# A fused attention and mixture-of-experts layer: squares stored head by head, and the first row maximum ahead of their sums

## What is computed

```python
h = layernorm(x) * (1 + ca) + sa              # ca, sa, ga, cb, sb, gb: per batch, from silu(c) @ wmod
Q, gate = split(h @ Wq + bq); K = h @ Wk + bk; V = h @ Wv + bv      # 16 heads of 8 features
Q = qn_w * Q * rsqrt(mean(Q*Q over a head's 8) + 1e-6); K likewise with kn_w
attn = softmax(Q @ K.T / sqrt(8)); o = (attn @ V) * sigmoid(gate)
x = x + ga * (o @ Wo + bo)
h = layernorm(x) * (1 + cb) + sb
x = x + gb * (top-2 of 32 experts, each a 128 x 128 matrix, weighted by the softmax of h @ router_w.T)
```

## Time and profile before

| what | us |
|---|---|
| median of 3 runs | 1000.58 |
| lowest, highest | 999.42, 1006.95 |
| the profiled execution | 1003.27 |
| its span in the profile | 1001.5 |
| VectorE busy in it | 741.2 |
| the square sums (L1103), 32 times | 32.5 |
| the row maxima (L1134), 512 times | 337.0 |

### The profile page before, as it was taken

One profiled execution on the slowest core, in us unless ns is written; L12 is line 12 of the kernel. 1 busy time (PEld: TensorE's weight loads), 2 busy tenths in 40 slices (PEclk: granted clock), 3 DMA queues, 4 the chain that ended last, 5 costly groups with the idle time before them and its releaser, 6 DMA issues. The chain is left out here.

```text
span 1001.5 us, 25119 instructions
## 1 busy us (share of the span) xinstructions
PE 650.4 (65%) x5838; PEld 412.3 (41%) x5839; DVE 741.2 (74%) x2240; ACT 539.7 (54%) x1335; POOL 545.1 (54%) x887
## 2 busy tenths in 40 slices
PE   3278798888889889888888888887187850000000
PEld 1135455555555545555554555554086740000000
DVE  8388799999999999999998999973334823334433
ACT  1247687777788878787877787875023320000000
POOL 7122255666566666666665666656600007677775
PEclk9569999999999999999999999998589995555555
DMA  2635564545444635454455445432188863444443
GB/s 70 189 86 142 129 155 127 157 119 141 123 124 125 141 112 138 122 142 118 122 133 130 121 119 137 116 97 62 35 262 273 271 210 89 111 115 104 115 115 89
DMA packets 128433, 132.33 MB, mean 132 GB/s; under 512 B 16900, under 2 KB 112868, under 8 KB 128388
## 3 DMA queue, kind: packets, MB, share of 16 engines
q1 hardware_dynamic: 100868, 95.81, 37.1%
q0 software_dynamic: 8192, 16.79, 6.2%
q10 hardware_dynamic: 19328, 19.20, 5.8%
HBM read 78.62 MB, written 52.56 MB: 131 GB/s over the span
## 5 line engine op out<-in xcount | busy, mean ns | idle before, releaser
L1134 DVE TENSOR_REDUCE negmax<-mx_ps 128x2 f32<-128x512 f32 x512 | 337.0, 682 | 25.2 <-PE mx_ps L1488 24.6
L884 ACT ACTIVATE pr<-st_ps 128x512 f32<-128x512 f32 x512 | 287.7, 596 | 41.9 <-PE st_ps L1512 41.7
L1488 PE MATMUL mx_ps<-k_aug,q_aug 126*128 126x256 bf16 x1024 | 195.4, 278 | 88.8 <-DVE negmax L1134 51.1
L748 POOL DMA_INDIRECT yg<-ys_d,gi x128 | 124.8, 975 | 147.6 <-DMA ys_d<-ys 101.9
L1512 PE MATMUL st_ps<-q_aug,k_aug 128*128 128x256 bf16 x1024 | 169.7, 273 | 0.9 <-ACT pr L884 0.4
L706 POOL DMA_INDIRECT xs_d<-h,slot x128 | 127.7, 998 | 55.8 <-DVE slot L1257 31.9
L1488 PEld LDWEIGHTS mx_ps<-k_aug,q_aug 126*128 126x128 bf16 x1024 | 75.2, 97 | 190.8 <-issue 182.2
L1526 PE MATMUL o_ps<-pr,v_aug 128*32 128x256 f32 x2048 | 138.8, 389 | 0.4 <-issue 0.4
L1512 PEld LDWEIGHTS st_ps<-q_aug,k_aug 128*128 128x128 bf16 x1024 | 92.0, 100 | 34.7 <-issue 12.6
L1388 DVE TENSOR_SCALAR yw<-yg,p_all 128x128 f32<-128x128 f32 x64 | 16.4, 314 | 113.7 <-DMA yg<-ys_d,gi 113.7
L1526 PEld LDWEIGHTS o_ps<-pr,v_aug 128*32 128x32 f32 x2048 | 53.9, 110 | 50.0 <-issue 28.4
(11 more groups left out here) (168 smaller groups left out, 1261.2 us busy)
## 6 DMA issues: line engine op xcount, KB each, us to landing
q_aug<-q_d SPq DMA_DIRECT2D x64, 192.0 KB
xs<-xs_d SPq DMA_DIRECT2D x96, 128.0 KB, 3.0
ys_d<-ys ACTq DMA_DIRECT2D x48, 256.0 KB, 3.0
mod_o<-mod_d SPq DMA_DIRECT2D x32, 256.0 KB, 4.8
bias_p<-bias_d SPq DMA_DIRECT2D x32, 200.0 KB, 4.8
q_d<-parts SPq DMA_DIRECT2D x32, 192.0 KB, 2.1
k_d<-parts SPq DMA_DIRECT2D x32, 192.0 KB, 2.1
k_aug<-k_d SPq DMA_DIRECT2D x64, 96.0 KB
```

The lines of the kernel that those rows point to most:

```text
L748: nc.gpsimd.indirect_dma_start(yg[:, par, k, :], None, ys_d, bass.IndirectOffsetOnAxis(ap=gi[:, par, k:k + 1], axis=0)).then_inc(yg_ld[par ...
L884: nc.scalar.activation(pr[:, h % PR], st_ps[score_bank(b, h)][:], ACT.Exp, scale=SCALE).then_inc(exp_d, 1)
L1134: v.tensor_reduce(negmax[:, :, h], mx_ps[h % 2][:], AX.X, ALU.max, negate=True).then_inc(mx_d, 1)
L1488: last = t_.matmul(mx_ps[h % 2][:, qc], q_aug[b.par][0:MROW, h, qc * P:(qc + 1) * P], k_aug[b.par][0:MROW, h, :], start=True, stop=True)
```

## The change

ScalarE squares the two halves of 128 tokens one by one, and writes a head's eight squares side by side: it reads Q and K as before and writes with a step of 8 elements (32 bytes) between neighbours. VectorE's sum then reads packed elements, and writes `ss` in the same order as before. In VectorE's order the first row maximum of the next batch stands in front of the sum instead of behind it. Nothing else moves.

```diff
             def squares(b):
                 wait(act, qkv_d, TB * (b.n + 1))
                 wait(act, ss_d, b.n)
-                nc.scalar.activation(sq[:], qkvg[:, b.par, :, 0:2 * P], ACT.Square).then_inc(sq_d, 1)
+                for t in range(TB):
+                    ins = nc.scalar.activation(sq[:, t].rearrange("p (k h d) -> p k d h", k=2, h=H),
+                                               qkvg[:, b.par, t, 0:2 * P].rearrange("p (k d h) -> p k d h", k=2, h=H), ACT.Square)
+                ins.then_inc(sq_d, 1)
...
             def square_sums(b):
                 wait(dve, sq_d, b.n + 1)
-                v.tensor_reduce(ss[:].rearrange("p (k h) -> p k h", h=H),
-                                sq[:].rearrange("p t (k d h) -> p (t k) h d", k=2, h=H), AX.X, ALU.add).then_inc(ss_d, 1)
+                v.tensor_reduce(ss[:],
+                                sq[:].rearrange("p t (g d) -> p (t g) d", d=HD), AX.X, ALU.add).then_inc(ss_d, 1)
...
                 ln2_stats(b4)
                 ln2_aggregate(b4)
+                max_head(b1, 0)
                 square_sums(b0)
-                max_head(b1, 0)
                 max_head(b1, 1)
                 rms_newton_a(b0)
```

## The result

| | before | after |
|---|---|---|
| median of 6 runs each, us | 1001.2 | 1016.54 |
| lowest, highest | 998.19, 1006.95 | 1015.16, 1021.73 |
| the profiled execution, its span | 1003.27, 1001.5 | 1021.73, 1019.6 |

The ratio of after to before is 1.0156, with a 95% interval of 1.0115 to 1.0197: the change makes the kernel slower by 1.6%. Forecast was 1020, with a range of 1001 to 1028, and a chance of 0.67 that it would be slower by over 1%.

What follows compares the result with a forecast made beforehand. The prediction took a ring through SP's list, the modulation rows' load and GpSimd's L627, L636, L599 as the bound. Early steps 6.7, caught steps 12.1 and tail 0.9 sum to 19.7 us, giving 1020 us, range 1001 to 1028.

Steps and rivals of the forecast that it cites:

- The sum itself: VectorE's square sum, once packed, takes 0.67 us instead of 1015 ns; bounds 0.60 and 1.015.
- The squares: ScalarE's two instructions take 0.8 us together, bounds 0.63 and 1.6; covered in the new order, 0.1 us per step without cover.
- The order: VectorE idles before the next batch's first maximum (start m), then sums; Newton at m+2.29 instead of m+1.21, 1.08 us later.
- The catch: Mid-step, GpSimd's L599 holds rstd and L577 the shift; 0.93 us per caught step, 13 of 21 steps, 12.1 us.
- GpSimd's load-bound train: L627 waits 2.59 us for the modulation rows' load, then L636 and L599 follow; VectorE's two-input instructions are held meanwhile.
- a shorter wait of L627 for its load: Sign of being wrong, on GpSimd: it would mean the SP list isn't what bounds the step.
- the ring: Loop's bounding cycle: last maximum, SP's list, load, L627, L636, L599, shift, seven maxima, last maximum; mean turn 19.7 us.
- Seven of them pass on 0.95 each, 6.7 us: Of the nine steps before 225 us, seven pass on the delay, 0.95 us each; two wait longer for loads.
- that the slack absorbs it: Rival: the waits mid-step take the delay, slower before 225 us only, 7.6 us, 1008.2 us; chance 0.24.
- that VectorE's busy time counts: Rival: VectorE is the bound, the order costs nothing and 10.9 us come off, 989.7 us; chance 0.09.
- That every step is caught: Rival: all 21 steps lose 0.93 us to GpSimd's holds, 27.1 us with the rest, 1027.7 us; chance 0.08.
- that the sum gets no shorter: Rival: outputs cost, not stride; delay 0.34 us longer, 18 steps caught, 27 us, 1027.6 us; chance 0.06.

Runs made afterwards that it cites:

- e1: The changed kernel with the sum put back in front of the first maximum, packed squares and sum kept: 1003.4 us, ratio to the kernel before 1.0047.
- e6: The kernel before with a dead VectorE reduction of 256 elements per step, a delay of 0.33 us: 1006.7 us, ratio 1.0032.
- e7: The kernel before with a dead VectorE reduction of 640 elements per step, a delay of 0.73 us: 1013.3 us, ratio 1.0127.
- e3: The kernel before with GpSimd's scaled input weights (L577) and low part (L599) moved ahead of x plus bias: 975.2 us, ratio 0.9779.
- e2: The kernel before with only the first maximum moved in front of the square sums, strided sum kept: 1022.1 us, ratio 1.0264.
- e5: The kernel before with the squares split into two instructions that write side by side, strided sum and old order: 999.2 us (one run).

## Why the prediction was right

- *The sum itself.* 0.67 us predicted, 0.676 measured. The neighbour with packed elements was the right one to scale from.
- *The squares.* 0.8 us taken for both, 1.14 measured, inside the bounds; covered in the new order as said. In the old order the price is 0.46 us of waiting, not 0.1, and e1 shows it.
- *The order.* Scores absent when the maximum's turn comes: idle 0.44 to 1.03 us in front of it in all of the 21 steps. Newton step at m+2.29 predicted, m+2.30 measured. After a caught step the scores come earlier: idle 0.44 to 0.47 us (0.59 once), against 0.66 to 1.03 after uncaught ones; 0.37 less was predicted.
- *The catch.* 0.93 us per caught step and 13 steps were predicted; 0.94 (from -0.06 to 0.88; in one step 1.52) and 11 were found. For a threshold e6 and e7 speak, that GpSimd's load-bound train is what holds VectorE is shown by e3, and that the order brings the catches by e1 and e2. That the number of steps is near owes something to luck: going through the distances of before again by the prediction's rule gives its 13 steps, and only seven of them are among the 11. The strict alternation wasn't foreseen.
- *A sign of being wrong that came.* The prediction named a shorter wait of L627 for its load as a sign that the ring doesn't hang on SP's list. The wait did get shorter, from 2.91 to 2.14 us in the mean of the 21 steps. The sign was badly chosen: from the store of the maximum rows to the issue of the load it is 5.19 us in before and 5.18 in after, and from there to L627 4.88 and 4.73. The load comes as before, and GpSimd gets to its wait later.
- *Mis-sized: "Seven of them pass on 0.95 each, 6.7 us".* The tenth maximum of the step after 225 us is late by only 2.5 us (238.7 against 236.2). It isn't passed on evenly: the tenth maximum is 3.3 us late at 96.5 us and 0.8 us late a step on, at 116.4. The delay ran into waits for loads that were there anyway. The first maximum between these two, in before and in after:

```profile
105.70 1.29 DVE L1134 TENSOR_REDUCE negmax<-mx_ps 128x2 f32<-128x512 f32 x2 [2.98 <-PE mx_ps L1488]
```

```profile
106.35 0.69 DVE L1137 TENSOR_REDUCE negmax<-mx_ps 128x2 f32<-128x512 f32 x1 [1.27 <-PE mx_ps L1491]
```

  1.7 us of lateness went into a wait of 2.98. I had allowed for two such steps; the 2.5 us that are left of 6.7 say that the waits took more.
- *Missing: the clock.* The loop from there on lost 13.9 us (395.8 to 409.8 over 20 steps), 12.1 were predicted. The catch explains 20 x 0.55 = 11.0. In 5 of the 11 caught steps VectorE waits another 1.1 to 1.3 us in front of the thirteenth maximum, four of them within these 20 steps (20 x 0.28 = 5.6 in all); the prediction didn't have that term. What it is stands in the last section. The two together are more than the loss; the load, 0.15 us sooner at L627, gives 3.0 back.
- *The sum.* 6.7, 12.1 and 0.9 us were predicted for the early steps, the loop and the tail, 19.7 in all; the spans have 2.5, 13.9 and 1.7, together 18.1, and the medians are 15.3 apart. A term too large and one that was missing partly cancel, so the total is nearer than its parts.

The rivals: that the slack absorbs it is refuted by 11 catches and by the interval's lower end, 1.0115; that VectorE's busy time counts, by e6, and by e1, which has 5 us less of it and is slower. That every step is caught, by the 10 that aren't; that the sum gets no shorter, by its 0.676 us.

## What to carry to other kernels

An engine that is busy nearly all the time can be held rather than working: look for short instructions whose mean is several times their minimum, and see with which instruction of another engine they end. Before an instruction is moved out of the place where it stands, ask what it covered there; a sum that fills a wait is free, and the same sum behind the wait costs its length and all that hangs on it. And a slack measured in the profile absorbs a delay only as long as the order in which two engines reach a shared resource stays as it is.

## What the hardware showed that I had not expected

**TensorE's clock fell behind short waits for VectorE.** Two stretches of the changed kernel, a caught step's and an uncaught one's (us, busy time by engine, then the granted clock as a share):

```profile
649.20:652.20 3.00, 2.93 (x21) 1.22 (x22) 1.81 (x6) 2.08 (x6) 1.14 (x3) 0.50 0.54 150
...
628.70:631.70 3.00, 2.95 (x34) 1.73 (x35) 3.00 (x8) 2.89 (x8) 1.36 (x4) 1.00 0.69 197
```

The granted clock is 0.50, so 1.2 GHz, in the first and 1.00, 2.4 GHz, in the second. Ahead of the fall TensorE waited for VectorE's maxima twice within 2.2 us, 1.03 and 0.94 us (the second of these is in the caught step's rows above). The product with V, sixteen matmuls, then takes 1.94 us instead of 1.07, and the maximum behind the next scores waits:

```profile
652.29 1.45 DVE L1137 TENSOR_REDUCE negmax<-mx_ps 128x2 f32<-128x512 f32 x2 [1.28 <-PE mx_ps L1491]
```

It happens in 5 steps after 225 us, with falls at 281, 362, 444, 526 and 649 us, all in caught steps, and in no step after 225 us of the profile before (that has two earlier ones, at 105 us, where TensorE waits 3.58 us for k_aug, and at 156 us, behind two waits for VectorE of 0.94 and 0.89). So a hold on VectorE can be paid twice, the second time on TensorE. A caught step isn't needed for it: of e7's two falls one, at 260 us, stands in an uncaught step, behind this wait:

```profile
259.17 0.38 PE L1491 MATMUL mx_ps<-k_aug,q_aug 126*128 126x256 bf16 x2 [1.66 <-DVE negmax L1135]
```
The Trainium skill, TensorE: Matmul & The Clock Gate, section HAM oscillation — how this bites in real kernels, tells of a clock that falls again and again because TensorE waits for transfers; the rows agree as to the fall, and here the wait was for another engine. It doesn't come with every such wait: six caught steps of the changed kernel have none (in the one at 567 us the two waits are 0.81 and 0.95 us), and e2, with 15 catches, has none after 225 us at all; why not stays open.

**Scattered writing on ScalarE, 32 bytes apart, cost more than scattered reading on VectorE, 64 bytes apart**: 1.05 ns more per element (e5 against the changed kernel) and 0.66 (before against the changed kernel). The Trainium skill, Advanced Engine Details and Errata, section SBUF Cachelines, says that accesses which follow each other in the same 16 bytes run at full performance, and that a different such line for each access is penalised; the rows agree for both engines, and put a number to each.
